# Query and output products on row halves of TensorE, maxima turned by VectorE

## The reference, cut to what matters

```
qh = (LN(x) @ Wq.T)      32 heads of 16
kh = (ctx @ Wk.T), vh = (ctx @ Wv.T)      8 groups of 16, each for 4 heads
out = softmax(qh kh^T / 4) vh
x  = x + tanh(g_xattn) * (out @ Wfc.T + bfc)
x  = x + tanh(g_ffn) * (shared(LN(x)) + comb_w * routed(LN(x)))
```

## Time and profile before

| | us |
|---|---|
| median of 3 runs (889.1 to 889.56) | 889.33 |
| the profiled execution | 890.05 |
| its span, first to last instruction | 887.7 |
| attention stage with its end, span time | 44.9 to 350 |

### The profile page before, as it was taken

How to read it: one execution, slowest core, us unless ns; L and a number is a source line. 1 busy time by engine, 2 the same in 40 slices (tenths; PEclk the granted TensorE clock), 3 DMA queues, 4 the chain that set the end, 5 groups by cost and what they waited for, 6 DMA issues and landing times.

```text
span 887.7 us, 14887 instructions
## 1 busy us (share of the span) xinstructions
PE 860.1 (97%) x4923; PEld 642.5 (72%) x4923; DVE 635.8 (72%) x1085; ACT 337.2 (38%) x636; POOL 477.8 (54%) x485
## 2 busy tenths in 40 slices
PE   8689999999999889999999999999999999999998
PEld 6445665665565447888888888888788888888886
DVE  7789899889889966666556655679665566656565
ACT  4186576667657852122112211344211121112111
POOL 2313004001203999787668666954966696678640
PEclk9889999999999999999999999999999999999999
DMA  7763342432432113121112111211311112111102
GB/s 274 232 175 105 127 121 61 149 116 78 131 107 74 38 28 93 48 72 47 47 47 71 47 47 47 72 47 65 115 59 48 47 52 66 47 47 47 47 1 95
DMA packets 43609, 71.88 MB, mean 81 GB/s; under 512 B 6064, under 2 KB 21936, under 8 KB 43312
## 3 DMA queue, kind: packets, MB, share of 16 engines
q1 hardware_dynamic: 43568, 71.34, 25.5%
HBM read 55.33 MB, written 15.73 MB: 80 GB/s over the span
## 4 chain that ended last, share of the span: by engine, by line
PE 84%; DVE 11%; issue 2%; ACT 1%; DMA 1%; SPq 0%; DVEq 0%; ACTq 0%
PE bank L1293 24%; PE bank L1295 23%; PE bank L1294 23%; DVE mcol L906 5%; PE bank L1353 4%; PE bank L1378 4%; PE bank L1368 3%; PE bank L1298 2%; PE bank L1399 1%; DVE oN L1038 1%; ACT probs L761 1%; DVE oB L1028 1%; DVE x_l L1256 1%; DVE aT_l L881 0%; DMA q_scr<-qx_l 0%
## 5 line engine op out<-in xcount | busy, mean ns | idle before, releaser
L1293 PE MATMUL bank<-x_l,w_h 128*128 128x512 f32 x504 | 197.3, 391 | 0.3 <-DVE c L1116 0.3
L1294 PE MATMUL bank<-x_h,w_l 128*128 128x512 f32 x504 | 196.2, 389 | 0.0
L1295 PE MATMUL bank<-x_h,w_h 128*128 128x512 f32 x504 | 196.2, 389 | 0.0
L906 DVE TENSOR_REDUCE mcol<-bank 128x2 f32<-128x512 f32 x256 | 164.7, 671 | 24.8 <-PE bank L1353 24.3
L620 ACT ACTIVATE hT_h<-bank 128x512 fp32r<-128x512 f32 x72 | 43.1, 599 | 355.9 <-DVE bank L1231 347.2
L761 ACT ACTIVATE probs<-bank 128x512 f32<-128x512 f32 x256 | 138.9, 596 | 73.3 <-PE bank L1368 71.7
L572 POOL TENSOR_TENSOR w_l<-raw,w_h 128x512 fp32r<-128x512 f32 (+1 forms) x144 | 161.9, 1157 | 2.9
L1128 DVE SCALAR_TENSOR_TENSOR xa<-bank,tgf,xa 128x512 f32<-128x512 f32 x128 | 96.2, 751 | 77.7 <-PE bank L1295 77.5
L1293 PE MATMUL bank<-dn_l,hT_h 128*128 128x512 f32 x288 | 112.0, 389 | 0.0
L1294 PE MATMUL bank<-dn_h,hT_l 128*128 128x512 f32 x288 | 112.0, 389 | 0.0
L1295 PE MATMUL bank<-dn_h,hT_h 128*128 128x512 f32 x288 | 112.0, 389 | 0.0
(11 more groups left out here) (149 smaller groups left out, 1340.6 us busy)
## 6 DMA issues: line engine op xcount, KB each, us to landing
raw<-w_gu SPq DMA_DIRECT2D x36, 512.0 KB, 3.3
dnraw<-w_dn SPq DMA_DIRECT2D x36, 256.0 KB, 2.6
q_st<-q_scr SPq DMA_DIRECT2D x64, 128.0 KB, 2.7
q_scr<-qx_h SPq DMA_DIRECT2D x16, 256.0 KB, 2.2
q_scr<-qx_l SPq DMA_DIRECT2D x16, 256.0 KB, 2.2
q_st<-q_scr SPq DMA_DIRECT2D x64, 64.0 KB, 2.7
out<-xa SPq DMA_DIRECT2D x16, 256.0 KB, 2.0
cx_raw<-ctxT SPq DMA_DIRECT2D x14, 256.0 KB, 3.0
```

Of the source, the lines that this page charges most:

```text
L906: v.tensor_reduce(at[:, :, qt], sm_bank(n, s, u)[:, :].rearrange("p (r k) -> p r k", r=2), AX.X, ALU.max).then_inc(max_ok, 1)
L1293: mm(out, a_h, b_l, start=start, stop=False, skip_group_check=onto)
L1294: mm(out, a_l, b_h, start=False, stop=False, skip_group_check=onto)
L1295: return mm(out, a_h, b_h, start=False, stop=stop, skip_group_check=onto)
```

## The change

- **Query products.** `q_both` makes two q chunks together. Each 128-row product is cut in two 64-row products that run on the two halves of the array's rows and write different banks: first "unturned" (rows 0 to 63 into PJ[0], rows 64 to 127 into PJ[1]), later "turned" (crosswise), so that each bank gets both halves. Between them TensorE waits for its own first half (`half_q`).
- **Output products.** `f_both` does the same for the two query tiles of a batch, in blocks 0 to 2; the last block and the work behind it keep `f_part`.
- **Order.** Fill is placed anew: f in steps 0, 1 and 6, 7, x jobs in steps 1 and 2, kv in steps 2 and 3, q in steps 3 to 6. Copies and low parts of x and q come two at a time. `f_sum` of a batch comes as two at once, those of batch half 0 in step 0 of the next block. v's transposes go to the second half of OTB and wait for `o_turn`.
- **Maxima.** VectorE turns `mcol` (now 128x32) with a 32x32 transpose in unit 0 (`turn_maxima`); the sign is in k_st's row (-1 instead of 1), and in the row of q_st with the maxima it is plus. TensorE's `mt_job` and ScalarE's `m_copy` go. `put_max` sends four DMAs (16 rows of 32) per step in place of two; `m_rd` is two semaphores.
- **GpSimd** makes `a_low` in blocks 0 to 2 (the last block's stay on VectorE).
- **Sync engine.** `write_q` sends two chunks in steps 4 and 6 in place of one in each of 4 to 7.

Of TensorE's body the last part of the diff shows the new lines alone; the lines that they replace stand in the kernel printed above.

```diff
+def f_bank(t, bb, qt, last):
+    alone = last and (bb == 1 if not (isinstance(t, int) and t == BLOCKS - 1) else bb == 0)
+    return PJ[1] if alone else PJ[qt]
+def vt_place(tb, bb):
+    if isinstance(tb, int) and (tb, bb) in ((0, 0), (BLOCKS - 1, 1)):
+        return PJ[(bb + 1) % 2][:, 0:S]
+    return OTB[:, S:2 * S]
...
 def put_max(n, slot):
-        sp.wait_ge(mt_cp, n + 1)
-        for e in range(2):
-            at = e * ROWS + MROW
-            sp.dma_start(r(q_st[at:at + 1, slot, :, :].rearrange("p h (t q) -> p (h t) q", q=P)),
-                         r(mT[e * HC:(e + 1) * HC, :])).then_inc(m_rd, 16)
+        sp.wait_ge(mt_ok, n + 1)
+        for j in range(4):
+            lot = 32 * j
+            sp.dma_start(r(q_st[MROW:MROW + ROWS + 1:ROWS, slot, :, :].rearrange("e h (t j q) -> e (h t) j q",
+                                                                               j=4, q=32)[:, :, j, :]),
+                         r(mT[lot:lot + 16, slot % 2, :])).then_inc(m_rd[slot % 2], 16)
...
-            if s >= 4 and not last:
+            if s in (4, 6) and not last:
                 write_q(t + 1, s - 4)
+                write_q(t + 1, s - 3)
...
+    def a_low(n, c, bb):
+        pool.wait_ge(a_hi, n + 1)
+        g.tensor_tensor(a_split[False][bb][:, c, :], aT[:, c % 2, :], a_split[True][bb][:, c, :].bitcast(f32),
+                        ALU.subtract).then_inc(a_lo, 1)
...
+            if not (first and s == 0):
+                a_low(n - 1, (s - 1) % CHUNKS, (s - 1) % STEPS // CHUNKS)
...
-                if u == 3 and (not last or s + 1 < STEPS):
-                    m_copy(n + 1)
...
-                    x_high(nx, 0)
                 if s == 0 and u == 7:
-                    x_high(nx, 1)
                     xn_tile(nx, 2)
                 if s == 1 and u in (1, 5):
                     cx_high(nx, u // 4)
                 if s == 1 and u == 3:
                     xn_tile(nx, 3)
-                    x_high(nx, 2)
-                if s == 1 and u == 7:
-                    x_high(nx, 3)
+                if (s, u) in ((1, 7), (2, 3)):
+                    x_high(nx, 2 * (s - 1))
+                    x_high(nx, 2 * (s - 1) + 1)
                 if (s, u) in ((2, 7), (3, 1)):
                     cx_high(nx, s)
-                if s == 3 and u == 7:
+                if s == 3 and u == 3:
+                    k_high(nx)
                     v_copy(nx)
-                    k_high(nx)
-                if (s, u) in ((4, 3), (5, 3), (6, 1), (7, 3)):
+                if s == 6 and u == 3:
+                    vt_copy(nx, 0)
+                if (s, u) in ((4, 7), (6, 3)):
                     q_high(nx, s - 4)
-                if s == 7 and u == 7:
-                    vt_copy(nx, 0)
+                    q_high(nx, s - 3)
...
+    def turn_maxima(n, par):
+        dve.wait_ge(max_ok, UNITS * (n + 1))
+        if not (isinstance(n, int) and n < 2):
+            dve.wait_ge(m_rd[par], 32 * (n - par))
+        v.transpose(mT[:, par, :].bitcast(f32),
+                    mcol[:, par, :].bitcast(f32)).then_inc(mt_ok, 1)
...
-    v.memset(k_st[:, :, :, :].bitcast(f32), 1.0).then_inc(consts, 1)
+    v.memset(k_st[:, :, :, :].bitcast(f32), -1.0).then_inc(consts, 1)
+    v.memset(mcol[:, :, :].bitcast(f32), 0.0)
...
-                if not last and (s, u) in ((1, 0), (2, 0)):
-                    x_low(nx, 2 * s - 1)
+                if u == 0 and (not last or s + 1 < STEPS):
+                    turn_maxima(n + 1, (s + 1) % 2)
+                if not last and (s, u) in ((2, 0), (2, 4)):
+                    x_low(nx, u // 2)
+                    x_low(nx, u // 2 + 1)
...
-                    if u == 7:
+                    if u == 7 and last:
                         a_low(n - 1, (s - 1) % CHUNKS, (s - 1) % STEPS // CHUNKS)
-                    if (s, u) in ((1, 3), (2, 4)):
-                        f_sum(t - 1, 1, s - 1)
-                    if s == 1 and u == 7:
-                        f_stats(t - 1, 0, 1)
-                    if s == 2 and u == 6:
-                        f_stats(t - 1, 1, 0)
-                    if s == 3 and u == 4:
-                        f_stats(t - 1, 1, 1)
+                    if s == 0 and u == 0:
+                        for qt in range(2):
+                            f_sum(t - 1, 0, qt, False)
+                    if (s, u) in (((1, 3), (2, 4)) if last else ((1, 5), (1, 6))):
+                        f_sum(t - 1, 1, s - 1 if last else u - 5, last)
+                    if (s, u) in (((0, 6), (1, 7)) if last else ((3, 4), (4, 4))):
+                        f_stats(t - 1, 0, s if last else s - 3)
+                    if (s, u) in (((2, 6), (3, 4)) if last else ((7, 3), (7, 6))):
+                        f_stats(t - 1, 1, s - 2 if last else u // 6)
...
-                if s in (6, 7) and u == 7:
-                    f_sum(t, 0, s - 6)
-                if s == 7 and u == 4:
-                    f_stats(t, 0, 0)
-                if s in (0, 1) and u == 5:
-                    x_low(nx, 2 * s)
-                if s == 4 and u == 1:
+                if s == 3 and u == 4:
                     k_low(nx)
-                if (s, u) in ((4, 5), (5, 5), (6, 3), (7, 5)):
-                    q_low(nx, s - 4)
+                if (s, u) in ((5, 0), (6, 4)):
+                    q_low(nx, 2 * (s - 5))
+                    q_low(nx, 2 * (s - 5) + 1)
...
+    def both(out, a_h, a_l, b_h, b_l, turned, start, stop):
+        last = [None, None]
+        for k, (a, b) in enumerate(((a_h, b_l), (a_l, b_h), (a_h, b_h))):
+            for e in range(2):
+                rows, i = slice(e * ROWS, (e + 1) * ROWS), 1 - e if turned else e
+                last[e] = mm(out[i], a(rows, i), b(rows, i), start=start and k == 0, stop=stop and k == 2,
+                             skip_group_check=True)
+        return last
+    def q_both(tb, o, chunks, turned, start=False, stop=False, done=None):
+        def weights(tile, c):
+            return lambda rows, i: tile[rows, c, (o + i) * P:(o + i + 1) * P]
+        def tokens(tile, c):
+            return lambda rows, i: tile[rows, c, :]
+        for c in chunks:
+            last = both((PJ[0][:, :], PJ[1][:, :]), weights(wq_h, c), weights(wq_l, c), tokens(xnT_h, c),
+                        tokens(xnT_l, c), turned, start and c == chunks[0], stop and c == chunks[-1])
+        for one in last if done else ():
+            one.then_inc(done, 1)
+    def f_both(t, bb, chunks, turned, start=False, stop=False, done=None):
+        def results(tile, c):
+            return lambda rows, i: tile[rows, c, i * P:(i + 1) * P]
+        def weights(tile, c):
+            return lambda rows, i: tile[rows, c, :]
+        for c in chunks:
+            pe.wait_ge(a_lo, STEPS * t + CHUNKS * bb + c + 1)
+            last = both((PJ[0][:, :], PJ[1][:, :]), results(a_split[True][bb], c), results(a_split[False][bb], c),
+                        weights(wfc_h, c), weights(wfc_l, c), turned, start and c == chunks[0],
+                        stop and c == chunks[-1])
+        for one in last if done else ():
+            one.then_inc(done, 1)
...
-                    pe.wait_ge(m_rd, 32 * (n + 1))
+                    pe.wait_ge(m_rd[s % 2], 32 * (n - s % 2) + 64)
+                if not first and not last and (s, v) == (1, 2):
+                    pe.wait_ge(half_f1, 4 * t)
+                    f_both(t - 1, 1, (3,), False, stop=True, done=f_mm)
+                if not last and (s, v) == (5, 2):
+                    q_both(nx, 2, (2, 3), False, done=half_q)
+                if not last and (s, v) == (7, 2):
+                    pe.wait_ge(half_f0, 2 * t + 2)
+                    f_both(t, 0, (0, 1), True)
-                    if not last or s + 1 < STEPS:
-                        pe.wait_ge(mt_cp, n + 2)
+                    if not last and s in (2, 6):
+                        pe.wait_ge(vt_cp, 2 * t + 2 + s // 6)
...
+                if not first:
+                    if s == 0 and v == 1:
+                        pe.wait_ge(f_add, TILES * t - 2)
+                        f_both(t - 1, 1, (0, 1, 2), False, start=True, done=half_f1)
+                    if s == 0 and v == 3:
+                        pe.wait_ge(half_f1, 4 * t - 2)
+                        f_both(t - 1, 1, (0, 1, 2), True)
+                    if s == 1 and v == 1:
+                        f_both(t - 1, 1, (3,), True, done=half_f1)
+                if s == 1 and v == 3:
                     if first:
                         pe.wait_ge(k_lo, 1)
                     else:
+                        pe.wait_ge(f_add, TILES * t)
                     x_job(nx, 0)
                     x_job(nx, 1)
                 if s == 2 and v == 1:
+                    pe.wait_ge(ob_ok, n)
                     vt_job(t, 1)
+                    for j in (2, 3):
+                        pe.wait_ge(x_lo, TILES * nx + j - 1)
+                        x_job(nx, j)
                 if s == 2 and v == 3:
```

(26 more changed lines are left out.)

122 lines of the change are left out of this document (26 added, 96 removed).

## The result

The changed kernel takes 895.9 us, median of 5 runs (894.05 to 897.53), beside 889.1 for the kernel before on the same chip: a ratio of 1.0083, interval 1.0071 to 1.0095, so slower by 0.8%. The forecast was 890.3 with a range of 880 to 899. The range held the time; the point was 5.6 us low, and the direction (a change within the noise) was not what came.

The account below looks back on a forecast made before the run. VectorE was taken to set steps 1 and 3 and the last block, TensorE most others. Blocks 1 and 2 +1.0, block 0 -2.6, last block +2.6 gave +1.0 us on the 889.33 median: 890.3, range 880 to 899.

Parts of the forecast that it names:

- TensorE's part: Attention stage: paired half products 0.23 us apart, 0.41 saved per slot of only such products; TensorE alone 71.8 to 66.4 per block.
- step 2: Block 1 or 2: v's transposes wait for o_turn, late low parts of x delay kv products; 10.8 us against 9.6.
- Step 4: Block 1 or 2: sync engine's four maxima DMAs, 0.68 us per issue, land at 9.4 us and delay the next scores.
- Step 5: Block 1 or 2: q's write and reads put the maxima DMAs late in the sync queue; landed at 9.7 us, not 8.4.
- step 6: Block 1 or 2: paired ScalarE copies delay two exponentials, 0.5 us each; forecast 8.9 us against 9.4 before.
- Step 0: Block 1 or 2: both f sums ahead of f_both cost 0.4 us, two ctx loads precede the maxima; 8.9 against 8.3.
- The last block: VectorE bounds it: two f sums (1.3), a statistic (0.6) and seven turns (1.0, less 0.3 idle) add 2.6 us.
- Block 0: First block: x transposes and low parts move out of its first two steps, later steps shorten; -2.6 us in sum.
- rival 4: Halved products: TensorE still drains between 49-row and 64-row use, losing 2 to 2.5 us per block; 897, chance 0.07.
- rival 2: Landing of the last maxima DMA sets nearly every step, 0.79 us per issue and 2.7 landing; +9, 899.3, chance 0.20.
- Rival 1: Three blocks: waits mostly stay covered and TensorE's gain comes through; half of some 20 us, 880.3, chance 0.27.
- rival 3: TensorE pairs: weight loads don't overlap on the same halves, 0.11 us dearer per pair, 29 us; 919, chance 0.03.

## Why the prediction was right or wrong

**TensorE's part: right.** Pairs at 0.227 (forecast 0.23), no pause behind the scores. A slot with nine pairs takes 2.52; the forecast's list gives 0.88 - 0.41 + 9 x 0.23 = 2.54. With six pairs it takes 1.85, forecast 1.85. Slots in which pairs stand beside probabilities times values save nothing, as costed.

**Steps of block 2: right to 0.5 in the sum, mixed in the parts.** Steps 1, 2, 3 came to 8.87, 10.62 and 9.33 (9.1, 10.8, 9.4). The reason for step 2 held in the one half that mattered: the low parts ending 7.5 into the step (measured 7.25) and the kv products behind them; the wait for `o_turn`, which I had named first, does not matter. Step 4 was 0.9 too high: the issues of the maxima cost 0.54, not 0.68, and the last of them was there before the scores. Step 5 was nearly right (9.50 for 9.7) for the wrong reason: with the queue freed of maxima it still takes 9.30. In the changed kernel its first two slots, behind the paired copies and low parts of q, take 2.08 and 2.26 where their matmuls need 1.66 and 1.85. The same on step 6, 9.28 for 8.9: I had costed each pair of copies at 0.5 and no pair of low parts. Step 0, 9.27 for 8.9: VectorE's list ahead of the pairs, 0.8 and not 0.4, whichever order it is in. Step 7, which was to be near 7.9, took 8.24.

**The last block: +1.8 for +2.6.** The forecast had sums and statistic in step 0; they show in steps 0 and 1 (9.10 and 9.39 for 7.80 and 8.70), and the five steps behind them come to 0.2 less together.

**Block 0: the step that failed.** The sum had -2.6 and "a clock that rises later would cost 0 to 2", of which it took 0. Measured +2.0. Step 1 was to be 1.3 shorter and was 1.7 longer, at a mean granted clock of 0.55 where before it had 1.00; step 0 was to be 1.6 shorter and was 0.3. Step 2 was 1.0 longer for 1.6, step 3 1.2 for 0.8, and steps 4 to 7 together 1.7 shorter for 2.1. The eight transposes of x were priced at half clock, 2.2 us; before, only four of them ran at half clock, and all eight took about 1.6 (from 47.76 to 48.75 and from 52.91 to 53.52, where the next scores start). And where that work went, the half clock lasted longer, which the sum had taken at nothing. With early matmuls in both kernels block 0 is 72.9 after and 72.8 before. So of the 4.6 us between forecast and measurement the clock makes about 1.9 (the fillers give block 0 3.4 us after and 1.5 before), within the 0 to 2 that the forecast had named, and some 2.7 are missing at full clock too. How much of that the fillers themselves take was not measured.

**Block 1: not in the forecast at all.** It copied block 2's sum. The queue's slack in step 5 is about zero, and in the profiled executions it came out late there in block 1, by 0.3 to 1.4 us, in one with half clock behind it: +2.8 in the changed kernel's.

**Rivals.** None came true as a mechanism. The time lies near rival 4 (897) and rival 2 (899), but pairs run without drains and the maxima's landing seldom sets a step. Rival 1's floor of waits that stay covered was the furthest off but for rival 3. That the time lies in the range is in good part luck: block 0 missed by 4.6 and block 1 by 2.3 on one side, the last block by 0.8, block 2 by 0.5 and the stage's start by 1.0 on the other, and the range was wide for the sake of rivals that did not come. Slower had a chance of 0.41, and is what happened; the likeliest single case was not.

By part, the change is: GpSimd's low parts -1.2; the maxima about 0 (block 2 -0.6); the halves -2.6 to -2.8 in block 2; and the order that gives the halves slots of their own, which costs 4.0 in block 2 and 1.8 in the last block.

## What to carry to other kernels

Price an order apart from the instruction it serves: here the better instruction (two 64-row products side by side, in slots of only such products) returned 2.8 us per block and its order took 4.0, and putting the cheap parts alone into the old order beat both. A wait shown in a row is worth removing only if the engine that ends it has idle time before that; VectorE without a gap up to the last low part meant that two reorderings moved time between slots and none away. Where TensorE comes out of a half-idle stretch at half clock, matmul work taken out of the next steps may cost more than it saves; look at the granted clock there first, and cost a stand at about twice its length where the clock is seen to drop with it (2.7 us cost 5.3 here). And compare the granted clocks of all runs before a single profile is read: two executions of the same list differed by 7 us of half clock.

## What was not expected of the hardware

- The clock fell with short stands: one of 2.7 us went with 6.8 us at 0.50, one of 3.6 (block 1 with the maxima first) with 3.4, and 2.80 us with 1.47 busy were followed by 3.4 us at 0.50. Stands of 1.2, 1.4 and 1.9 us at the end of step 5 (q's writes first, block 2; sums first, block 1; maxima first, block 2) were not followed by a drop. The Trainium skill, page "TensorE: Matmul & The Clock Gate", Part 1, says that the throttled state is the default and activity releases it, and its table has two levels; the trace agrees, with every stretch here at 0.50 or 1.00 or a mean of the two.
- A 128x32 transpose on VectorE takes 0.20 recorded; one of 128x256 takes 0.45. An eighth of the size is not an eighth of the time.
- The same subtraction of 128x256 takes 0.73 us on GpSimd and 0.43 on VectorE.
- GpSimd's issue of the four maxima DMAs takes 2.24 us, the sync engine's 2.16. I had feared it much slower; what it cost was the work that stood behind it.
